# Corner sums of two samples in one GpSimd operation, and fewer comparisons on ScalarE, in the deformable stage of a metaformer kernel

## Chip, cores and metric

The kernel runs on one core of one Trainium2 chip. The metric is the device time of one execution in microseconds; the median of several runs is given. The engines are TensorE (PE in the profile; PEld is its weight load), VectorE (DVE), ScalarE (ACT), GpSimd (POOL) and SyncE (SP), each with its own queue of instructions; they wait for each other by semaphores.

## Reference

The model has four blocks, each a convolutional mixer and a feed-forward part, on x of shape (8, 64, 16, 16). The change lies in the mixer of the second block, a deformable convolution:

```
y = _layernorm(x)
h = conv3x3(y, w1) + b1;  offset = conv3x3(h, w2) + b2        # 4 groups x 9 taps x (dy, dx)
py = dy + ky + row;  px = dx + kx + column                    # sampling points
val = gather(y0, x0) * (wy0 * wx0) + gather(y0, x0 + 1) * (wy0 * wx1) \
    + gather(y0 + 1, x0) * (wy1 * wx0) + gather(y0 + 1, x0 + 1) * (wy1 * wx1)
x = x + relu(einsum('ogck,bgckhw->bohw', wr, val))
```

There are 4 groups x 9 taps = 36 sampling points ("samples") for each of the 8 x 256 = 2048 pixels, and each sample takes 16 channels at its 4 corners. Everything before and after this stage is the same in both kernels.

## The kernel before, in words

The 2048 pixels are 16 tiles of 128 (TILES = 16). A gather is made by TensorE as a matrix product with a one-hot matrix: for each sample, the index of its upper left corner (0 to 255, of an image's 256 pixels) is broadcast to all 128 partitions as a row of 2048 numbers (BC, four buffers, copied by SyncE from DRAM, L890), and compared with the partition's number. One comparison makes the one-hot for pixels 0 to 127 (the lower, qh = 0), another for pixels 128 to 255 (the upper, qh = 1); OH has three buffers (NOH = 3) of both.

- VectorE, `compare(s)` (L1095 to L1101), makes the lower comparison of each sample, and both where s % 3 is 0. One comparison is one tensor_scalar (is_equal) of 128 x 2048 fp16.
- ScalarE makes the upper comparison where s % 3 is 1 or 2, in two activations: DIST = |BC - q| (L1037) and OH = relu(1 - DIST) (L1040). `scalars(s)` is the number of samples up to s that ScalarE makes, and the value of the semaphore scalar_oh for which TensorE, SyncE and ScalarE wait.
- TensorE, `gather(s)` (L945 to L959), multiplies: 64 matmuls for a sample into two PSUM banks (4 and 5, or 6 and 7, by s % 2). It waits for the one-hots and for weigh(s - 2), which frees the banks.
- VectorE, `weigh(s)` (L1103 to L1112), multiplies the gathered values by the corner weights, two tensor_tensor of 128 x 512 from PSUM, into U, a pair of buffers (the tensors SQ and SD) by s % 2. It waits for gather(s) and, for the buffer, for GpSimd's sum of sample s - 2.
- GpSimd adds the four corners in two steps for each sample: V (V1, L903), 512 elements in each partition, then VAL (L906), 256 elements.
- After each eight samples TensorE transposes VAL in `contract` (L975), ScalarE evacuates it to VTA in `evac` (L1029), and TensorE multiplies it by the weights wd in `project` (L984). contract(n) stands after gather(11), (19), (27), (35), with contract(4) at the end; evac(n) stands on ScalarE after sample 13, 21, 29, and at the end.

Each engine's order is written out by hand. VectorE's is: compare(0), compare(1), the corner weights, then for s = 0 to 35: compare(s + 1) (not for s = 0), weigh(s). TensorE's is: gather(s), with contract and project where named. ScalarE can run ahead of the gathers by the three buffers of OH (its second activation waits for gather(s - 3)); SyncE refills BC(s) once both comparisons of sample s - 4 are made.

Of the kernel before, what the change touches and what calls it, by code (L numbers as in the profile page):

```python
# [11 lines left out]
ALU = mybir.AluOpType  # L12
ACT = mybir.ActivationFunctionType
F32 = mybir.dt.float32
# [5 lines left out]
P = 128  # L20
# [3 lines left out]
COLS = NB * PIX  # L24
HC = COLS // 2
TILES = B * PIX // P
# [7 lines left out]
SAMPLES = 36  # L34
CG = 16
# [37 lines left out]
def build(nc, x_dram, packs, idx_dram, out_dram):  # L73
    with ExitStack() as ctx:
        def sb(name, shape, dt=F32, where=None):
            return (where or ctx).enter_context(nc.sbuf_tensor(name, shape, dt))
# [3 lines left out]

        X = sb("X", [P, COLS])
        Y = sb("Y", [P, COLS])
        SQ = sb("SQ", [P, COLS])
        SD = sb("SD", [P, COLS])

        wconst = sb("wconst", [P, WIDTH[0]])
        wbuf = [sb(f"wbuf{i}", [P, max(w for n, w in enumerate(WIDTH) if n and n % 2 == i)]) for i in range(2)]
# [3 lines left out]
        def bank(n, cols=512):  # L91
            return PS[:, n * 512:n * 512 + cols]

        def wt(name, a=0, n=None, p0=0, p1=P):
            s, at, cols = AT[name]
            n = cols - a if n is None else n
            return wsb[s][p0:p1, at + a:at + a + n]
# [26 lines left out]
        def after_pool(eng, ins):  # L124

            steps["pool"] += 1
            ins.then_inc(pool_step, 1)
            eng.wait_ge(pool_step, steps["pool"])
# [13 lines left out]
        def ln_pe(pe, n):  # L142
            for h in range(2):
                pe.matmul(bank(h), wt("center"), X[:, h * HC:(h + 1) * HC], start=True, stop=True).then_inc(ln_centered, 1)  # L144
            for h in range(2):
                pe.wait_ge(ln_squared, 2 * n + h + 1)
                for q in range(4):
                    mm = pe.matmul(bank(2 + h, P)[32 * q:32 * q + 32, :], wt("mean32"), SQ[:, h * HC + q * P:h * HC + (q + 1) * P],
                                   start=True, stop=True, tile_position=(0, 32 * q))
                mm.then_inc(ln_var, 1)  # L150
            for h in range(2):
                pe.wait_ge(ln_rstd, 2 * n + h + 1)
                for q in range(4):
                    mm = pe.matmul(bank(2 + h)[:, q * P:(q + 1) * P], wt("spread", q * P, P), SD[:, h * P:(h + 1) * P],  # L154
                                   start=True, stop=True)
                mm.then_inc(ln_spread, 1)

        def ln_act(act, n, eps):
            if n == 0:
                warm(act, ACT.Sqrt)  # L160
            for h in range(2):
                act.wait_ge(ln_centered, 2 * n + h + 1)
                act.activation(SQ[:, h * HC:(h + 1) * HC], bank(h), ACT.Square).then_inc(ln_squared, 1)  # L163
            for h in range(2):
                act.wait_ge(ln_var, 2 * n + h + 1)
                act.activation(SD[:, h * P:(h + 1) * P], bank(2 + h, P), ACT.Sqrt, bias=wt(eps)).then_inc(ln_sd, 1)

        def ln_dve(dve, n, out_of):
# [6 lines left out]
            for h in range(2):  # L175
                c = slice(h * P, (h + 1) * P)
                dve.wait_ge(ln_sd, 2 * n + h + 1)
                dve.reciprocal(SD[:, c], SD[:, c]).then_inc(ln_rstd, 1)  # L178
            for h in range(2):
# [8 lines left out]
        def images(a):  # L188
            return a.rearrange("p (b r w) -> p b r w", b=2, r=H)
# [18 lines left out]
        with ExitStack() as sctx, nc.Block() as block:  # L208
# [60 lines left out]
            @block.sync  # L269
            def _(sp):  # L270
                xv = x_dram.rearrange("(g b) c p -> g c b p", g=2)
                for g in range(2):
                    sp.dma_start(X[C * g:C * g + C, :].rearrange("c (b p) -> c b p", b=NB), xv[g]).then_inc(x_in, 16)
                for n in range(3):
                    load_weights(sp, n)
# [557 lines left out]
        with ExitStack() as sctx, nc.Block() as block:  # L833
# [23 lines left out]

            def scalars(s):

                return s - s // 3  # L860
            BC = sb("BC", [P, NBC, TILES * P], FP16, sctx)
            OH = sb("OH", [P, NOH, 2, TILES * P], FP16, sctx)
            DIST = sb("DIST", [P, TILES * P], FP16, sctx)
            scalar_oh = sem("s3_scalar_oh")

            U = [a[:, :].rearrange("p (t k c) -> p t k c", t=TILES, k=4) for a in (SQ, SD)]
            V1 = sb("V1", [P, TILES, 2, CG], F32, sctx)
            VAL = sb("VAL", [P, 2, TILES, 8, CG], F32, sctx)
            (y_pad, c1_ps, h_in, tents_ready, c2_ps, gx_ps, gx_hi, gx_done, idx_ready, frac_ready, idxt_ps, idxt_in, idx_out,
             oh_ready, ga_ps, u_ready, val_ready, vt_ps, vt_in, dc_ps, xs_ready) = (  # L870
# [24 lines left out]
            @block.gpsimd  # L895
            def _(pool):
                pool.memset(YP[:, :, :], 0.0).then_inc(y_pad, 1)
                for k in range(3):
                    pool.memset(HS3[k][:, :, :], 0.0).then_inc(y_pad, 1)
                for s in range(SAMPLES):  # L900

                    pool.wait_ge(u_ready, s + 1)
                    after_pool(pool, pool.tensor_tensor(V1[:, :, :, :], U[s % 2][:, :, 0:2, :], U[s % 2][:, :, 2:4, :], ALU.add))  # L903
                    if s >= 16 and s % 8 == 0:
                        pool.wait_ge(vt_ps, 4 * (s // 8 - 1))
                    pool.tensor_tensor(VAL[:, (s // 8) % 2, :, s % 8, :], V1[:, :, 0, :], V1[:, :, 1, :], ALU.add).then_inc(val_ready, 1)  # L906
                    pool.wait_ge(val_ready, s + 1)

            @block.tensor
            def _(pe):  # L910
# [88 lines left out]
            @block.scalar  # L999
            def _(act):  # L1000
                ln_act(act, 2, "epsc")
                act.wait_ge(w_in[3], 16)
                act.wait_ge(y_pad, 4)
                for h in range(2):
                    act.wait_ge(c1_ps, h + 1)
                    for k in range(3):

                        a, b = max(0, 1 - k), min(W, W + 1 - k)
                        act.activation(pair(HS3[k], h, 2, 0)[:, :, :, a:b], images(bank(4 + h))[:, :, :, a + k - 1:b + k - 1],
                                       ACT.Identity, bias=wt("c1b")).then_inc(h_in, 1)  # L1010
                for n in range(2 * NB):
                    bl, qh = n // 2, n % 2
                    act.wait_ge(gx_ps, n + 1)
                    act.activation(GX[:, 0, qh, bl, :, :], bank(n % 4).rearrange("p (k c) -> p k c", k=4), ACT.Copy,
                                   scale=GSCALE).then_inc(gx_hi, 1)
                for g in range(NB):
                    act.wait_ge(idxt_ps, g + 1)
                    act.activation(IDXT[:, g * HC:(g + 1) * HC], bank(g).bitcast(FP16)[0:SAMPLES, 0:HC], ACT.Copy).then_inc(idxt_in, 1)

                act.wait_ge(frac_ready, 1)  # L1020
                for u, at in ((U0, 0.0), (U1, -1.0)):
                    after_act(act, act.activation(u[:, :, :], PY[:, :, :], ACT.Abs, bias=at if at == 0.0 else wt("minus1")))
                    act.activation(u[:, :, :], u[:, :, :], ACT.Relu, bias=1.0, scale=-1.0).then_inc(tents_ready, 1)

                def evac(ch):
                    rows = P if ch < 4 else 64
                    for q in range(4):
                        act.wait_ge(vt_ps, 4 * ch + q + 1)
                        act.activation(VTA[0:rows, ch % 4, q * 512:(q + 1) * 512], bank(q % 2)[0:rows, :], ACT.Copy).then_inc(vt_in, 1)  # L1029
                for s in range(SAMPLES):  # L1030

                    if s % 3:
                        act.wait_ge(bc_in[s % NBC], 16 * (s // NBC + 1))
                        if scalars(s - 1):

                            act.wait_ge(scalar_oh, scalars(s - 1))
                        after_act(act, act.activation(DIST[:, :], BC[:, s % NBC, :], ACT.Abs, bias=wt("negq1")))  # L1037
                        if s >= NOH:
                            act.wait_ge(ga_ps, s - NOH + 1)
                        act.activation(OH[:, s % NOH, 1, :], DIST[:, :], ACT.Relu, bias=1.0, scale=-1.0).then_inc(scalar_oh, 1)  # L1040
                    if s >= 13 and s % 8 == 5:
                        evac(s // 8 - 1)
                evac(3)
                evac(4)

                warm(act, ACT.Sqrt)

            @block.vector
            def _(dve):
# [7 lines left out]
                for n in range(2 * NB):  # L1057
                    bl, qh = n // 2, n % 2
# [10 lines left out]
                for g in range(NB):  # L1069
                    t = slice(4 * g, 4 * g + 4)  # L1070
# [24 lines left out]
                def compare(s):  # L1095
                    dve.wait_ge(bc_in[s % NBC], 16 * (s // NBC + 1))
                    if s >= NOH:
                        dve.wait_ge(ga_ps, s - NOH + 1)
                    for qh in range(1 if s % 3 else 2):
                        ins = dve.tensor_scalar(OH[:, s % NOH, qh, :], BC[:, s % NBC, :], wt("qidx", qh, 1), None, ALU.is_equal)  # L1100
                    ins.then_inc(oh_ready, 1)  # L1101

                def weigh(s):  # L1103
                    dve.wait_ge(ga_ps, s + 1)
                    if s >= 2:
                        dve.wait_ge(val_ready, s - 1)
                    for half in range(2):
                        o = U[s % 2][:, 8 * half:8 * half + 8, :, :].rearrange("p t k c -> p (t k) c")
                        src = bank(4 + 2 * (s % 2) + half).rearrange("p (k c) -> p k c", c=CG)
                        w = WC[:, s, 8 * half:8 * half + 8, :].rearrange("p t (k o) -> p (t k) o", o=1).broadcast_to([P, 32, CG])  # L1110
                        ins = dve.tensor_tensor(o, src, w, ALU.mult)  # L1111
                    ins.then_inc(u_ready, 1)  # L1112
# [8 lines left out]
                for bp in range(2):  # L1121
                    c = slice(bp * HC, (bp + 1) * HC)
# [900 lines left out]
```

## Time and profile before

| | us |
|---|---|
| median of 3 runs | 659.53 |
| lowest, highest | 659.16, 660.15 |
| the profiled execution | 663.59 |
| its span in the profile | 661.8 |

Times in the rows are microseconds from the start of the span unless marked ns. A timeline row gives start, duration, engine, line, operation, written tile <- read tiles, shapes, how many instructions were merged into the row (x2), and in brackets the idle time of the engine before it with what ended it. The page's second section shows the same as slices; the profiled execution is 4.1 us longer than the median of the plain runs, and the stage in question is about 122 us of it.

### The profile page before, as it was taken

What the parts mean: (1) busy time and instruction counts of PE and PEld (TensorE: products, weight loads), DVE (VectorE), ACT (ScalarE), POOL (GpSimd) and SP (SyncE); (2) the same over time, 40 slices, a digit from 0 to 9 for tenths busy, and PEclk for the clock granted to TensorE, in tenths of its full rate; (3) what the DMA queues carried; (4) which work ended last, traced back from release to release, by engine and by line L of the source; (5) the groups of instructions that cost most, each with busy time, mean ns of one, the idle gap of its engine ahead of it and who ended that gap; (6) DMA issues with size and microseconds to landing.
All of it is one profiled execution on the core that took longest, in us unless ns stands there. A gap on an engine that the chain in (4) does not pass through costs nothing. (4 is left out here: it accounts for less than half of the span.)

```text
span 661.8 us, 11669 instructions
## 1 busy us (share of the span) xinstructions
PE 555.0 (84%) x4942; PEld 297.8 (45%) x4942; DVE 352.8 (53%) x579; ACT 288.3 (44%) x395; POOL 148.6 (22%) x148
## 2 busy tenths in 40 slices
PE   3999999977899998487887867767997888799994
PEld 1544367844322467477777733233333334322221
DVE  2439902045455334787875837565235696632434
ACT  2633122223653231899998746443662011233221
POOL 9800000002000200298886920006003002000000
PEclk9999999999899999789997997796899999799998
DMA  7000000002000000655553100100002000000000
GB/s 270 2 2 2 1 0 1 0 1 93 1 0 1 29 0 10 221 195 171 195 183 130 66 16 1 45 8 30 0 0 104 0 0 1 0 1 1 0 17 16
DMA packets 7844, 30.09 MB, mean 45 GB/s; under 512 B 864, under 2 KB 2032, under 8 KB 7408
## 3 DMA queue, kind: packets, MB, share of 16 engines
q1 hardware_dynamic: 7792, 29.34, 12.7%
q8 instruction: 39, 0.64, 0.4%
q14 instruction: 13, 0.11, 0.0%
HBM read 28.67 MB, written 0.67 MB: 44 GB/s over the span
## 5 line engine op out<-in xcount | busy, mean ns | idle before, releaser
L958 PE MATMUL PS<-GX,OH 128*128 128x64 f16 x2304 | 76.0, 197 | 24.0 <-DVE OH L1100 16.1
L958 PEld LDWEIGHTS PS<-GX,OH 128*128 128x128 f16 x2304 | 73.9, 101 | 28.3 <-DVE OH L1100 19.5
L1037 ACT ACTIVATE DIST<-BC,wbuf 128x2048 f16<-128x2048 f16 x24 | 48.0, 2001 | 5.1 <-DMA BC<-idx_dram 3.3
L1821 DVE TENSOR_SCALAR HID<-PS,wbuf 128x512 f32<-128x512 f32 x32 | 23.8, 750 | 48.5 <-PE PS L1720 48.5
L1040 ACT ACTIVATE OH<-DIST 128x2048 f16<-128x2048 f16 x24 | 45.9, 1911 | 1.7 <-PE PS L958 1.0
L1100 DVE TENSOR_SCALAR OH<-BC,wbuf 128x2048 f16<-128x2048 f16 x48 | 42.6, 911 | 5.5 <-DMA BC<-idx_dram 5.5
L903 POOL TENSOR_TENSOR V<-SQ 128x512 f32<-128x512 f32 x18 | 27.5, 1527 | 67.9 <-DVE SQ L1111 66.8
L399 PE MATMUL PS<-T,DG 128*32 128x512 f32 x384 | 41.6, 593 | 0.7 <-DVE T L604 0.7
L144 PE MATMUL PS<-X,wconst 128*128 128x512 f32 x32 | 20.9, 786 | 22.6 <-DMA wconst<-pack_dram 8.9
L610 DVE SCALAR_TENSOR_TENSOR D<-QKVP,wbuf,D 128x1024 f32<-128x1024 f32 x27 | 34.5, 1285 | 8.9 <-ACT D L524 8.1
L163 ACT ACTIVATE SQ<-PS 128x512 f32<-128x512 f32 x16 | 9.6, 597 | 66.5 <-PE PS L144 66.5
L906 POOL TENSOR_TENSOR VAL<-V 128x256 f32<-128x256 f32 x36 | 37.0, 1027 | 2.8
L1760 ACT ACTIVATE HID<-PS,wbuf 128x512 f32<-128x512 f32 x32 | 21.9, 684 | 34.9 <-PE PS L1720 34.2
L1731 PE MATMUL PS<-HID,wbuf 128*64 128x512 f32 x128 | 36.1, 617 | 1.0 <-DVE HID L1821 1.0
L1716 PE MATMUL PS<-Y,wbuf 64*128 64x512 f32 x128 | 36.0, 639 | 0.7 <-ACT OMASK L1754 0.7
L1111 DVE TENSOR_TENSOR SQ<-PS,WC 128x512 f32<-128x512 f32 x36 | 23.1, 684 | 18.3 <-PE PS L958 16.2
L826 DVE TENSOR_TENSOR HS<-PS,HID 128x512 f32<-128x512 f32 x32 | 20.5, 686 | 20.0 <-PE PS L711 20.0
L690 POOL MEMSET CWT<- 128x2048 f32 x1 | 1.8, 1806 | 123.1 <-POOLq L208 123.1
L903 POOL TENSOR_TENSOR V<-SD 128x512 f32<-128x512 f32 x18 | 26.4, 1467 | 3.5 <-DVE SD L1111 2.3
L778 ACT ACTIVATE HID<-PS,wbuf 128x512 f32<-128x512 f32 x32 | 20.1, 682 | 14.0 <-PE PS L703 13.9
L399 PEld LDWEIGHTS PS<-T,DG 128*32 128x32 f32 x384 | 13.5, 110 | 27.8 <-issue 27.8
L388 PE MATMUL PS<-wbuf,D 128*128 128x256 f32 x96 | 25.7, 411 | 0.0
(304 smaller groups left out, 997.5 us busy)
## 6 DMA issues: line engine op xcount, KB each, us to landing
BC<-idx_dram SPq DMA_DIRECT2D x36, 512.0 KB, 4.0
wbuf<-pack_dram SPq DMA_DIRECT2D x1, 2468.0 KB, 11.8
wbuf<-pack_dram SPq DMA_DIRECT2D x1, 1656.0 KB, 7.2
wbuf<-pack_dram SPq DMA_DIRECT2D x1, 1494.5 KB, 6.1
wbuf<-pack_dram SPq DMA_DIRECT2D x1, 820.0 KB, 13.3
wbuf<-pack_dram SPq DMA_DIRECT2D x1, 732.0 KB, 3.9
wbuf<-pack_dram SPq DMA_DIRECT2D x1, 602.5 KB, 3.8
wconst<-pack_dram SPq DMA_DIRECT2D x1, 567.5 KB, 6.6
```

Source lines behind the costliest of these rows:

```text
L388: pe.matmul(half, src, w, start=(j == 0), stop=False)
L399: mm = pe.matmul(bank(DBANK[j] + n)[32 * q:32 * q + 32, :], DG[:, (2 * j + hf) * NBLK + i, :], src, start=(i == blocks[0]), stop=(i == blo ...
L610: ins = dve.scalar_tensor_tensor(out=d, in0=window(QKVP[j], dy, dx), scalar=wt("dw5", j * 25 + 5 * dy + dx, 1), in1=d, op0=ALU.mult, op1=A ...
L903: after_pool(pool, pool.tensor_tensor(V1[:, :, :, :], U[s % 2][:, :, 0:2, :], U[s % 2][:, :, 2:4, :], ALU.add))
L906: pool.tensor_tensor(VAL[:, (s // 8) % 2, :, s % 8, :], V1[:, :, 0, :], V1[:, :, 1, :], ALU.add).then_inc(val_ready, 1)
L958: mm = pe.matmul(o, OH[:, s % NOH, qh, t * P:(t + 1) * P], src, start=(qh == 0 and part == 0), stop=(qh == 1 and part == 1))
L1037: after_act(act, act.activation(DIST[:, :], BC[:, s % NBC, :], ACT.Abs, bias=wt("negq1")))
L1040: act.activation(OH[:, s % NOH, 1, :], DIST[:, :], ACT.Relu, bias=1.0, scale=-1.0).then_inc(scalar_oh, 1)
L1100: ins = dve.tensor_scalar(OH[:, s % NOH, qh, :], BC[:, s % NBC, :], wt("qidx", qh, 1), None, ALU.is_equal)
L1716: pe.matmul(bank(2 + (n + bh) % 4), wt("w1_3", e * FH3 + m * P, P, r, r + C), Y[r:r + C, bp * HC:(bp + 1) * HC], start=True, stop=False, t ...
L1731: pe.matmul(bank(bp)[C * bh:C * bh + C, :], wt("w2_3", (2 * e + m) * C, C), HID[:, (n + i) % 4, :], start=(e == 0 and m == 0), stop=False) ...
L1821: dve.tensor_scalar(HID[:, n % 4, :], bank(2 + n % 4), wt("b1_3", 2 * e + m, 1), 0.0, ALU.add, ALU.max).then_inc(hid_in_v, 1)
```

## The change

GpSimd's sums are made for two samples in one operation: `BATCHES` is (0, 2), (2, 2), ..., (32, 2), (34, 1), (35, 1). V of a batch of two has 1024 elements in each partition and VAL 512. For this U has two buffers of two samples each (SQ and SD, now one tensor SQSD, and a new tensor U_1) and V1 is twice as large. GpSimd waits for weigh of the later sample of its batch; weigh(s) waits for the batch before the last to be summed. The division of the upper comparisons goes from s % 3 to s % 5: VectorE makes both comparisons where s % 5 is 0 or 3 (15 samples instead of 12), ScalarE the upper one of the other 21 (instead of 24).

```diff
-        SQ = sb("SQ", [P, COLS])
-        SD = sb("SD", [P, COLS])
+        SQSD = sb("SQSD", [P, 2 * COLS])
+        SQ, SD = SQSD[:, 0:COLS], SQSD[:, COLS:2 * COLS]
...
-                return s - s // 3
+                return sum(1 for i in range(s + 1) if i % 5 not in (0, 3))
...
-            U = [a[:, :].rearrange("p (t k c) -> p t k c", t=TILES, k=4) for a in (SQ, SD)]
-            V1 = sb("V1", [P, TILES, 2, CG], F32, sctx)
+            U = [SQSD[:, :].rearrange("p (s t k c) -> p s t k c", s=2, t=TILES, k=4), sb("U_1", [P, 2, TILES, 4, CG], F32, sctx)]
+            V1 = sb("V1", [P, 2, TILES, 2, CG], F32, sctx)
+            BATCHES = [(s, 2) for s in range(0, SAMPLES - 2, 2)] + [(SAMPLES - 2, 1), (SAMPLES - 1, 1)]
...
-                for s in range(SAMPLES):
-
-                    pool.wait_ge(u_ready, s + 1)
-                    after_pool(pool, pool.tensor_tensor(V1[:, :, :, :], U[s % 2][:, :, 0:2, :], U[s % 2][:, :, 2:4, :], ALU.add))
+                for s, n in BATCHES:
+                    u = U[s // 2 % 2][:, s % 2:s % 2 + n].rearrange("p s t k c -> p (s t) k c")
+                    v = V1[:, 0:n].rearrange("p s t k c -> p (s t) k c")
+
+                    pool.wait_ge(u_ready, s + n)
+                    after_pool(pool, pool.tensor_tensor(v, u[:, :, 0:2, :], u[:, :, 2:4, :], ALU.add))
                     if s >= 16 and s % 8 == 0:
                         pool.wait_ge(vt_ps, 4 * (s // 8 - 1))
-                    pool.tensor_tensor(VAL[:, (s // 8) % 2, :, s % 8, :], V1[:, :, 0, :], V1[:, :, 1, :], ALU.add).then_inc(val_ready, 1)
-                    pool.wait_ge(val_ready, s + 1)
+                    v = V1[:, 0:n].rearrange("p s t k c -> p t s k c")
+                    pool.tensor_tensor(VAL[:, (s // 8) % 2, :, s % 8:s % 8 + n, :], v[:, :, :, 0, :], v[:, :, :, 1, :],
+                                       ALU.add).then_inc(val_ready, n)
+                    pool.wait_ge(val_ready, s + n)
...
-                    if s % 3:
+                    if s % 5 not in (0, 3):
...
-                    for qh in range(1 if s % 3 else 2):
+                    for qh in range(2 if s % 5 in (0, 3) else 1):
...
-                    if s >= 2:
-                        dve.wait_ge(val_ready, s - 1)
+                    if s >= 4:
+                        dve.wait_ge(val_ready, s // 2 * 2 - 2)
                     for half in range(2):
-                        o = U[s % 2][:, 8 * half:8 * half + 8, :, :].rearrange("p t k c -> p (t k) c")
+                        o = U[s // 2 % 2][:, s % 2, 8 * half:8 * half + 8, :, :].rearrange("p t k c -> p (t k) c")
```

## Rows read from the trace of the kernel before

**Rows 1.** The page: its span and the engines' busy times.
```profile
span 661.8 us, 11669 instructions
PE 555.0 (84%) x4942; PEld 297.8 (45%) x4942; DVE 352.8 (53%) x579; ACT 288.3 (44%) x395; POOL 148.6 (22%) x148
```
**Rows 2.** Slices of the stage: engines' busy us (instructions), then granted clock, DMA.
```profile
core 0: us, PE busy (x) PEld busy (x) DVE busy (x) ACT busy (x) POOL busy (x), PEclk, DMA share, GB/s
270.00:300.00 30.00, 23.52 (x671) 22.94 (x672) 26.82 (x37) 28.68 (x15) 21.50 (x17) 0.88 0.59 205
300.00:330.00 30.00, 23.58 (x649) 21.18 (x644) 23.90 (x35) 28.74 (x20) 26.16 (x21) 1.00 0.50 178
330.00:360.00 30.00, 23.27 (x580) 21.06 (x581) 20.77 (x29) 28.10 (x20) 24.09 (x20) 0.93 0.50 179
```
**Rows 3.** Groups by line, 269 to 392 us: busy, mean ns, idle before.
```profile
L958 PE MATMUL PS<-GX,OH 128*128 128x64 f16 x2304 | 76.0, 197 | 24.0 <-DVE OH L1100 16.1 <-ACT OH L1040 5.9 <-issue 2.0
...
L906 POOL TENSOR_TENSOR VAL<-V 128x256 f32<-128x256 f32 x36 | 37.0, 1027 | 2.8
```
**Rows 4.** ScalarE's timeline: first pairs, third evacuation, its waits, last activation.
```profile
270.44 2.00 ACT L1037 ACTIVATE DIST<-BC,wbuf 128x2048 f16<-128x2048 f16 x1 [2.04 <-DMA BC<-idx_dram]
...
274.48 2.00 ACT L1037 ACTIVATE DIST<-BC,wbuf 128x2048 f16<-128x2048 f16 x1
...
355.67 1.06 ACT L1029 ACTIVATE VTA<-PS 128x512 f32<-128x512 f32 x2
...
361.79 1.91 ACT L1040 ACTIVATE OH<-DIST 128x2048 f16<-128x2048 f16 x1 [0.99 <-PE PS L958]
...
369.01 2.00 ACT L1037 ACTIVATE DIST<-BC,wbuf 128x2048 f16<-128x2048 f16 x1 [1.27 <-DMA BC<-idx_dram]
...
375.08 1.91 ACT L1040 ACTIVATE OH<-DIST 128x2048 f16<-128x2048 f16 x1
```
**Rows 5.** VectorE's timeline, from windows of different width (x1 first, x2 both).
```profile
289.71 1.29 DVE L1111 TENSOR_TENSOR SD<-PS,WC 128x512 f32<-128x512 f32 x2 [0.60 <-PE PS L958]
...
295.28 0.74 DVE L1100 TENSOR_SCALAR OH<-BC,wbuf 128x2048 f16<-128x2048 f16 x1
...
295.28 1.89 DVE L1100 TENSOR_SCALAR OH<-BC,wbuf 128x2048 f16<-128x2048 f16 x2
...
317.79 1.29 DVE L1111 TENSOR_TENSOR SD<-PS,WC 128x512 f32<-128x512 f32 x2 [0.69 <-POOL VAL L906]
...
338.94 1.17 DVE L1100 TENSOR_SCALAR OH<-BC,wbuf 128x2048 f16<-128x2048 f16 x1
...
338.94 2.86 DVE L1100 TENSOR_SCALAR OH<-BC,wbuf 128x2048 f16<-128x2048 f16 x2
...
379.92 1.29 DVE L1111 TENSOR_TENSOR SD<-PS,WC 128x512 f32<-128x512 f32 x2 [0.87 <-POOL VAL L906]
```
**Rows 6.** GpSimd's timeline: additions beside comparisons, and the last ones, alone.
```profile
295.37 1.26 POOL L906 TENSOR_TENSOR VAL<-V 128x256 f32<-128x256 f32 x1
...
317.77 1.27 POOL L903 TENSOR_TENSOR V<-SQ 128x512 f32<-128x512 f32 x1
...
338.83 0.73 POOL L906 TENSOR_TENSOR VAL<-V 128x256 f32<-128x256 f32 x1
339.64 1.61 POOL L903 TENSOR_TENSOR V<-SQ 128x512 f32<-128x512 f32 x1
...
382.06 1.25 POOL L903 TENSOR_TENSOR V<-SD 128x512 f32<-128x512 f32 x1
383.39 0.73 POOL L906 TENSOR_TENSOR VAL<-V 128x256 f32<-128x256 f32 x1
```
**Rows 7.** TensorE's timeline: a gather at each clock, and an idle time.
```profile
270.64 3.40 PE L958 MATMUL PS<-GX,OH 128*128 128x64 f16 x64 [7.80 <-DVE OH L1100]
...
302.75 2.03 PE L958 MATMUL PS<-GX,OH 128*128 128x64 f16 x64 [1.61 <-ACT OH L1040]
...
356.31 1.97 PE L975 MATMUL PS<-wconst,VAL 128*128 128x128 f32 x8 [2.72 <-ACT VTA L1029]
```
**Rows 8.** Groups of GpSimd over the whole span: its longest addition.
```profile
L320 POOL TENSOR_TENSOR D<-wbuf,BK 96x768 f32<-96x768 f32 x1 | 1.5, 1539 | 0.1
```
**Rows 9.** The page's DMA issues: KB each, us to landing.
```profile
BC<-idx_dram SPq DMA_DIRECT2D x36, 512.0 KB, 4.0
```

## The prediction, made before the changed kernel was timed

> **What bounds the kernel now.** Everything that is changed lies in one stage, the deformable convolution, from about 269 to 391 us of a span of 661.8 us [rows 1]; so the first look is at the busy time of each engine in slices of that stage. ScalarE is busy 28.7 of 30 us there, GpSimd 26.2, TensorE 23.6, VectorE 23.9 [rows 2]. The second look is ScalarE's own timeline: from 270.44 it starts a comparison (a DIST and an OH activation) every 4.04 us, 24 of them, broken by three evacuations of VTA, to 377.0 (375.08 + 1.91) [rows 4]. 24 x 4.04 = 97.0 us; the evacuations take 2.3, 2.6 and 3.1; it waits 0.99 and 1.27 us; together 105 to 106.5 us. It is full, and sets the pace of the stage: 106.5 / 36 = 2.96 us for each sample. Lines say the same from the other side: the matmuls of the gather are only 76.0 us busy and wait 24.0 us for one-hots [rows 3].
>
> The third look is at what lies right behind ScalarE. GpSimd makes a sample's sums in 1.25 us (V) and 0.73 us (VAL) where it is alone, yet the mean VAL is 1027 ns [rows 3, 6]. The timelines of VectorE and GpSimd side by side show why. A comparison of VectorE (L1100) takes 0.74 us at 295.28; a second follows at once and the pair takes 1.89, not 1.41 us [rows 5]. The VAL of GpSimd issued at 295.37 took 1.26 us, to 296.63 [rows 6], and VectorE's second comparison could only finish 0.54 us later, at 297.17. At 338.94 both kinds of wait are seen: the first comparison takes 1.17 us since VAL is under way until 339.56; then V, issued at 339.64, holds to 341.25, and the second comparison ends at 341.80, 0.55 us later [rows 5, 6]. The reading: a comparison of VectorE and an addition of GpSimd exclude each other for their whole length, and GpSimd, if it stands waiting when the first of two comparisons ends, goes ahead of the second. There are 12 double comparisons; sample 0's, before GpSimd starts, takes 1.41 us, and each of the other 11 takes 1.88 us or more, with GpSimd's addition between the two. The weighing (L1111, from PSUM) isn't touched: 1.29 us for its two instructions at 317.79, beside a V of 1.27. The Trainium skill, "SBUF — State Buffer", section "Who interferes with whom", states this as a rule: the first of the two to issue holds the shared pair for its whole instruction. The rows agree, and what it does to the change is the forecast below.
>
> **The change part by part.**
> ScalarE: samples with s % 5 in 1, 2, 4 instead of s % 3 in 1, 2, that is 21 pairs instead of 24: 3 x 4.04 = 12.1 us less on the engine that sets the pace [rows 4].
> VectorE: three comparisons more, 51 instead of 48: 3 x 0.67 (0.74 less the overlap of neighbours) = 2.0 us, before waits.
> GpSimd: 17 batches of two samples and two of one. An addition costs 0.73 us for 256 and 1.25 for 512 elements: 0.2 fixed and 2.05 to 2.1 ns for each element [rows 6]. So V of 1024 is 2.35 us and VAL of 512 is 1.27: 3.6 for two samples instead of 3.96, and two gaps of 0.08 fewer, 17 x 0.5 = 9 us less. The trace has no addition of 1024; the nearest, 768 elements, took 1539 ns [rows 8], which gives at least 2.05 us; from above, no fixed part saved, 2.5 us. I take 2.35, which the two sizes of this very line give. Without its start of some 0.15, V keeps VectorE's comparison out for 2.2 us instead of 1.1, and VAL for 1.15 instead of 0.57. The Trainium skill, "GPSIMD Engine Reference", section "3.1 Elementwise", has 4497 ns for 2048 elements, an estimate of 2.25 us for 1024; the sum would be some 1 us lower by it.
> The waits: weighing s now needs the batch before the last (two buffers of two samples), always done in time by the schedule below, which removes the 0.69 us waits on VAL [rows 5]. The copy BC(s) for s % 5 = 1 starts after ScalarE's sample s - 4, now one pair (4.04 us) ahead instead of two, against 4.0 us to land [rows 9]: 0 to 0.5 us each on ScalarE, hidden while ScalarE isn't the last.
>
> **The schedule.** VectorE's order is compare(s + 1), then weigh(s). I laid the samples with the durations above (weigh 1.20, gather 1.95 at the full clock [rows 7], pair 4.04), following each wait. Sample 3 shows the pattern: weigh(1) ends and releases the batch (0,1) while the first comparison of sample 3 runs; V of 2.2 us takes its turn behind it, and only then comes the second: a double comparison takes 3.44 us instead of 1.8. gather(3), its weighing and all behind it are late by 1.6 us. So it is for each odd double sample (3, 5, 13, 15, ...). For an even one (8, 10, 18, ...) V is mostly in flight when the first comparison comes (0.7 to 1.0 us), and VAL goes between the two (1.15): 3.0 to 3.2 us. Both kinds in the times of the schedule, samples 7 to 10: weigh(7) 297.7 to 298.9; comparison 9 at 298.9, so V(6,7), released at 299.0, holds 299.6 to 301.8; gather(8) ends 299.8, weigh(8) to 301.0; the first comparison of 10 waits from 301.0 to 301.8 and ends 302.4; VAL(6,7) holds to 303.5; the second ends 304.1; gather(10) 304.1 to 306.1, when weigh(9) (304.0), comparison 11 (305.2) and V(8,9) behind it (305.9 to 308.2) have already begun, into which comparison 12 runs at 307.3.
> Ten samples on VectorE: weighing 12.0; six single comparisons, four of 0.67, one of 0.77 and one of 1.3, together 4.75; two odd doubles 6.9; two even 6.2; waits for a gather's end 1.1: 31.0 us. ScalarE would need 6 x 4.04 + 1.25 x 2.3 = 27.1 for the same ten, GpSimd 18 + its waits for 14 comparisons of 0.56, or 26.7. So VectorE's chain of weighing, blocked comparison and gather becomes the bound.
> Before, weigh(5) began at 289.71, weigh(15) at 317.79 and weigh(35) at 379.92 [rows 5]: 90.2 us for thirty, 30.1 for ten. Now: weigh(5) at 291.3, thirty samples at 31.0 = 93.1, weigh(35) at 384.4, 4.5 us later. GpSimd then ends 3.5 us behind it (the last two batches are single), before 4.2 (383.39 + 0.73 - 379.92) [rows 6]. The end of the stage moves by 4.5 - 0.7 = 3.8 us. What follows (contract(4), the projection) is the same.
> The clock: the schedule is at the full clock. Before, the granted clock of slices was 0.88 and 0.93 [rows 2]; a gather takes 3.40 us at the half clock, 2.03 at the full one [rows 7], and the clock fell after TensorE idled for 2.72 us. ScalarE's two waits and its long third evacuation, 3.1 us, are what that cost. Now TensorE idles for 2.4 to 2.9 us at about every fifth sample, so I expect such falls at least as often; half the gathers lie on the chain: 2 us, between 0 and 6.
> Sum: 3.8 + 2.0 = 5.8 us. The profiled execution took 663.59 (span 661.8), the runs' median is 659.53; the difference goes onto the median: 665.3 us.
>
> **The rivals.**
> A, the change pays as the busy times suggest. Place: the comparison next to V. If VectorE's second comparison isn't kept waiting by the longer addition, VectorE's ten samples fall from 31.0 by two times 2.1 and two times some 1 to below 25, and ScalarE's 27.1 decides: it ends at 270.44 + 84.8 + 8 = 363.2 to 364.5, the tail adds 9.8 (gather(33) ends with the last pair, weigh(33) 1.2, a batch 3.8 and 0.5 of waiting, two single batches of 2.16), so 374 against 384.1: 9.6 us faster, 649.9. It decides once the waits of ten samples (8.3 us) fall by 3.9, that is V's hold from 2.2 to about 1.4 us. For it: ScalarE is the full engine now. Against it: every double comparison of the trace. 12%.
> B, it comes out even: V nearer to 2.05 (2 us less), fewer falls of the clock (2 us less), and some even doubles meeting no V (1.65 instead of 3.1 us, as one did in my schedule). 657.5 to 660.8, 14%.
> C, TensorE's idle times let its clock fall in nearly every period: each fall puts 1.4 us on a gather [rows 7], four to seven of these on the chain instead of the 1.4 that I count: 669 to 673. 12%.
> The forecast itself, 662 to 668.5: 62%.
> That the change doesn't do what it says is no case here: its operands are plain.
>
> **How the numbers follow.** The likeliest case gives 665.3. Leaving out A and the upper end of C leaves 657.5 to 670. A measurement of this kernel can tell about 0.2% (1.3 us) from no change. Faster by more: A and a quarter of B, 0.16; within: 0.10; slower: the rest, 0.74.
>
> **What would show it.** In the trace after: V at 2.35 us alone and about 2.8 behind a comparison; the second comparison of samples 3, 5, 13, 15 at 2.85 us; ScalarE with waits on gathers instead of being full; "DVE OH" as the releaser of the gathers with more than 16 us; GpSimd no busier than 85 us; its last VAL near 388 to 390. Wrong if those comparisons take 0.75 to 1.3 us, or if ScalarE is full again and ends near 364.

## The result

| | ratio to the kernel before | 95% interval | median us, runs |
|---|---|---|---|
| changed kernel | 1.0146 | 1.0100 to 1.0192 | 671.93, 4 (before: 659.84) |
| once more, other comparison | 1.0147 | 1.0119 to 1.0176 | 671.6, 6 (before: 661.21) |

The change makes the kernel slower by 1.5%. On the 659.53 us from which the prediction started, 1.0146 is 669.2 us: within its range (657.5 to 670), 0.8 us below the upper end; the median of the four plain runs itself, 671.93, lies above it. The profiled execution took 670.25 us, span 668.5, against 663.59 and 661.8 before. One of the six executions of the second row was in a slower state (677.83 us, granted clock 0.940), and its ratio leaves it out.

The times of the four plain runs of the changed kernel go with the clock that TensorE was granted, as a mean over the run: 668.31 and 670.25 us at 0.949 and 0.947, 673.61 and 674.67 us at 0.939 and 0.937.

The page of the changed kernel: engines' busy time.

```profile
PE 556.3 (83%) x4942; PEld 298.2 (45%) x4942; DVE 373.1 (56%) x582; ACT 276.6 (41%) x389; POOL 133.7 (20%) x114
```

The repetition was made because the first interval is wide:

> The changed kernel itself, beside the others of this call on the same chip. Its first interval reached from 1.01 to 1.019 times the kernel before; by the others so far (V in two 1.0025, batches alone 1.0091) I expect 1.013 to 1.017.

In the busy times above ScalarE has 11.7 us less and GpSimd 14.9 us less to do than in [rows 1], as intended; VectorE has 20.3 us more. (A comparison or an addition that is kept out counts as busy while it waits.) The slices of the stage (columns as in [rows 2]) and the groups of lines between 266 and 400 us show which instruction has it:

```profile
270.00:300.00 30.00, 21.14 (x597) 20.48 (x595) 28.74 (x33) 25.53 (x14) 13.79 (x7) 0.90 0.53 175
300.00:330.00 30.00, 23.26 (x580) 21.16 (x576) 24.59 (x30) 22.77 (x15) 19.40 (x10) 0.89 0.48 162
330.00:360.00 30.00, 24.71 (x650) 21.56 (x647) 28.07 (x35) 23.60 (x16) 19.10 (x10) 0.94 0.47 160
```

```profile
L963 PE MATMUL PS<-GX,OH 128*128 128x64 f16 x2304 | 79.4, 200 | 33.9 <-DVE OH L1105 30.1 <-ACT OH L1045 2.6 <-issue 1.1
L1105 DVE TENSOR_SCALAR OH<-BC,wbuf 128x2048 f16<-128x2048 f16 x51 | 63.4, 1268 | 5.2 <-DMA BC<-idx_dram 5.1
L1042 ACT ACTIVATE DIST<-BC,wbuf 128x2048 f16<-128x2048 f16 x21 | 42.0, 2001 | 12.9 <-DMA BC<-idx_dram 11.9
```

The 51 comparisons of VectorE take 63.4 us, 1268 ns each, where before 48 took 42.6 us, 911 ns each (neighbours overlap a little, so the busy time is less than the sum); the gathers wait 30.1 us for them, in [rows 3] 16.1. ScalarE is no longer full: 22.8 to 25.5 us of 30 instead of 28.7.

The place itself, in the timelines of VectorE and GpSimd: a double comparison (both halves of a sample, on VectorE) behind the weighing of an odd sample (at 318 us), one behind the weighing of an even sample (at 301 us), and GpSimd's additions beside them.

```profile
300.74 2.98 DVE L1105 TENSOR_SCALAR OH<-BC,wbuf 128x2048 f16<-128x2048 f16 x2
...
317.74 0.74 DVE L1105 TENSOR_SCALAR OH<-BC,wbuf 128x2048 f16<-128x2048 f16 x1
...
317.74 3.49 DVE L1105 TENSOR_SCALAR OH<-BC,wbuf 128x2048 f16<-128x2048 f16 x2
```

```profile
292.78 2.40 POOL L906 TENSOR_TENSOR V<-SQSD 128x1024 f32<-128x1024 f32 x1 [2.76 <-DVE SQSD L1116]
...
301.63 1.54 POOL L910 TENSOR_TENSOR VAL<-V 128x512 f32<-128x512 f32 x1
...
317.97 2.70 POOL L906 TENSOR_TENSOR V<-SQSD 128x1024 f32<-128x1024 f32 x1 [2.42 <-DVE SQSD L1116]
```

The first comparison at 317.74 takes 0.74 us. V, issued at 317.97, ends at 320.67, and the second comparison ends at 321.23, 0.56 us after it. At 300.74 V is under way until 301.50, and VAL (301.63 to 303.17) goes between the two comparisons: 2.98 us. All eight doubles behind an odd weighing take 3.47 to 3.52 us, where [rows 5] show 1.89.

The chain that the page reports lies in the last stage, as before, and says nothing of this one.

### The profile page after: what moved, and what is told of

It reads as the page before. It is cut to its first block and busy times, and to the rows that moved or that the text cites. A ratio compares the mean times of both kernels' runs of the same rounds, so it can differ in the third digit from the quotient of the medians.

```text
span 668.5 us, 11621 instructions
## 1 busy us (share of the span) xinstructions
PE 556.3 (83%) x4942; PEld 298.2 (45%) x4942; DVE 373.1 (56%) x582; ACT 276.6 (41%) x389; POOL 133.7 (20%) x114
## 5 line engine op out<-in xcount | busy, mean ns | idle before, releaser
L963 PE MATMUL PS<-GX,OH 128*128 128x64 f16 x2304 | 79.4, 200 | 33.9 <-DVE OH L1105 30.1
L963 PEld LDWEIGHTS PS<-GX,OH 128*128 128x128 f16 x2304 | 76.7, 103 | 38.8 <-DVE OH L1105 34.4
L1105 DVE TENSOR_SCALAR OH<-BC,wbuf 128x2048 f16<-128x2048 f16 x51 | 63.4, 1268 | 5.2 <-DMA BC<-idx_dram 5.1
L1042 ACT ACTIVATE DIST<-BC,wbuf 128x2048 f16<-128x2048 f16 x21 | 42.0, 2001 | 12.9 <-DMA BC<-idx_dram 11.9
L1045 ACT ACTIVATE OH<-DIST 128x2048 f16<-128x2048 f16 x21 | 40.1, 1910 | 4.3 <-PE PS L963 3.7
L906 POOL TENSOR_TENSOR V<-SQSD 128x1024 f32<-128x1024 f32 x9 | 24.2, 2691 | 76.4 <-DVE SQSD L1116 76.4
L163 ACT ACTIVATE SQSD<-PS 128x512 f32<-128x512 f32 x16 | 9.6, 597 | 66.2 <-PE PS L144 66.2
L906 POOL TENSOR_TENSOR V<-U 128x1024 f32<-128x1024 f32 (+1 forms) x10 | 24.4, 2444 | 19.3 <-DVE U L1116 19.3
L910 POOL TENSOR_TENSOR VAL<-V 128x512 f32<-128x512 f32 (+1 forms) x19 | 27.3, 1437 | 2.6
L1116 DVE TENSOR_TENSOR U<-PS,WC 128x512 f32<-128x512 f32 x36 | 23.1, 681 | 7.9 <-PE PS L963 7.9
```

Of the source, the lines that this page charges most:

```text
L906: after_pool(pool, pool.tensor_tensor(v, u[:, :, 0:2, :], u[:, :, 2:4, :], ALU.add))
L910: pool.tensor_tensor(VAL[:, (s // 8) % 2, :, s % 8:s % 8 + n, :], v[:, :, :, 0, :], v[:, :, :, 1, :], ALU.add).then_inc(val_ready, n)
L963: mm = pe.matmul(o, OH[:, s % NOH, qh, t * P:(t + 1) * P], src, start=(qh == 0 and part == 0), stop=(qh == 1 and part == 1))
```

## The experiments

Each was timed in five rounds beside the kernel before, in three comparisons. "Stage" is the time from the first weighing to the second update of X in one profiled execution: 114.5 us before (275.86 to 390.37), 123.9 in the changed kernel (275.06 to 398.99). These 9.4 us agree with the ratio (9.6 us); the spans of the two profiled executions differ by only 6.7 us, since 2.7 us come out of stretches ahead of and behind the stage, in which nothing was changed. Differences in microseconds are taken from the ratios, on 659.53 us.

**The batches alone.** The old division (12 samples with both comparisons on VectorE), sums of two samples.

```diff
-                    if s % 5 not in (0, 3):
+                    if s % 3:
```

> The changed kernel with the old division of the upper comparisons (12 samples with both on VectorE, 24 on ScalarE); only GpSimd's batches of two stay. Theory (the longer hold of V keeps the second comparison of a double out): doubles are 11 behind GpSimd's start instead of 14, each still 2.4 to 3.5 us, so about 3 x 2 = 6 us less than the changed kernel, 662 to 666, still slower than before; doubles behind weigh of an odd sample still take 3.5 us. Rival (the three more comparisons on VectorE do the harm): at or under the time of before, 659 or less, since GpSimd has less to do.

Measured: 1.0091 (1.0068 to 1.0113), 6.0 us slower than before. A comparison of VectorE takes 1174 ns:

```profile
L1105 DVE TENSOR_SCALAR OH<-BC,wbuf 128x2048 f16<-128x2048 f16 x48 | 55.3, 1174 | 5.4 <-DMA BC<-idx_dram 5.4
```

So the larger part of the loss, 6.0 of 9.7 us, comes with the batches alone and not with VectorE's three more comparisons; 665.5 us is within the expectation. Six of its twelve doubles take 3.48 to 3.51 us, as the eight behind an odd weighing do in the changed kernel. The remaining 3.7 us come with the three more doubles; the expectation had put some 6 us on them.

**The division alone.** The kernel before with s % 5 in its three places, sums of one sample.

> The kernel before with only the division s % 5 (15 doubles on VectorE, 21 samples on ScalarE); GpSimd sums each sample by itself. Theory: doubles stay at 1.9 us, GpSimd's additions and all comparisons together take 36 x 2.16 + 51 x 0.56 = 106 us, against 105 before, so nothing is gained from the 12 us taken off ScalarE and little is lost: 658 to 663. Rival (the division does the harm): 665 or more. Second rival (ScalarE alone was the bound): 650 to 654.

Measured: 0.9952 (0.9928 to 0.9976), and in the repetition:

> The kernel before with the division s % 5 alone, once more, since its gain (0.9952, 0.9928 to 0.9976) is small. Expected 0.993 to 0.998.

0.9948 (0.9926 to 0.9970): faster than both kernels, by 3.3 us. A comparison takes 915 ns, as before, though three more are made, the stage 110.2 us:

```profile
L1100 DVE TENSOR_SCALAR OH<-BC,wbuf 128x2048 f16<-128x2048 f16 x51 | 45.4, 915 | 5.6 <-DMA BC<-idx_dram 5.6
```

The rival that the division does harm has fallen. I had expected 658 to 663 us and no gain, since GpSimd's additions and all comparisons together come to 106 us; 0.9952 is 656.4 us, so that was a miss. A part of ScalarE's 12.1 us is gained, 3.3 of them.

The traces show where. VectorE's weighings waited 16.8 us for gathers before and 7.5 in the division alone; against these 9.3 us stand 1.2 us more of waits for VAL and 2.8 us more of comparisons. That leaves 5.3 us, and from the first to the last weighing it is 98.7 us instead of 104.1. The longest single wait before, 6.65 us, was behind the third evacuation of VTA, for which TensorE waited 2.72 us [rows 7]; in the division alone TensorE waited 1.28 us for it, and the same weighing 1.69 us:

```profile
361.73 1.29 DVE L1111 TENSOR_TENSOR SQ<-PS,WC 128x512 f32<-128x512 f32 x2 [6.65 <-PE PS L958]
```

About 1 us of this is lost again behind the last weighing, 11.6 us to the end of the stage instead of 10.5.

The half of the change that takes load off the full engine pays by itself; the batches cost 6.0 us by themselves and 13 on top of the division.

**V of a batch in two additions.** Same wait for two samples, same VAL of 512; only the one addition of 1024 is now two of 512.

```diff
-                    after_pool(pool, pool.tensor_tensor(v, u[:, :, 0:2, :], u[:, :, 2:4, :], ALU.add))
+                    for i in range(n):
+                        w = slice(TILES * i, TILES * i + TILES)
+                        ins = pool.tensor_tensor(v[:, w], u[:, w, 0:2, :], u[:, w, 2:4, :], ALU.add)
+                    after_pool(pool, ins)
```

> The changed kernel with V of a batch made by two additions of 512 elements instead of one of 1024, under the same wait; VAL stays one of 512. Theory (the length of one hold is what counts): the second comparison of a double behind an odd weighing takes 1.7 us instead of 2.8, 8 times, so 8 to 10 us less than the changed kernel: 659 to 663. Rival (the late release, waiting for two samples, does the harm): no better than the changed kernel, 669 or more, since GpSimd's work grows by 17 x 0.2 us.

Measured: 1.0025 (1.0005 to 1.0045), 8 us less than the changed kernel, with one more addition in each batch for GpSimd. The eight doubles behind an odd weighing take 2.40 to 2.43 us instead of 3.47 to 3.52, here that of sample 15 (V is two additions merged into one row):

```profile
313.13 2.41 DVE L1108 TENSOR_SCALAR OH<-BC,wbuf 128x2048 f16<-128x2048 f16 x2
313.36 3.32 POOL L908 TENSOR_TENSOR V<-SQSD 128x512 f32<-128x512 f32 x2 [0.57 <-DVE SQSD L1119]
```

The second comparison gets its turn after the first of the two additions (1.1 us) and not after both. So the length of one addition accounts for 8 of the 13 us that the batches cost on top of the division. The rival, that the late release of a batch does the whole harm, has fallen; 5 us against the division alone (1.0025 and 0.995) are left, and this run doesn't say what they are due to.

**TensorE's idle times filled.** The changed kernel with 40 small matmuls ahead of the gathers of eleven double samples (not 0, 3, 20 and 28), into a PSUM bank that is free then; they are in no result.

```diff
+                    if s >= 5 and s % 5 in (0, 3) and s % 8 != 4:
+                        if s >= 12:
+                            pe.wait_ge(vt_in, 4 * ((s - 12) // 8 + 1))
+                        for _ in range(FILL):
+                            pe.matmul(bank(0)[:, 0:64], IDH[:, :], GX[:, 0, 0, 0, :, 0:CG], start=True, stop=True)
                     pe.wait_ge(oh_ready, s + 1)
```

> The changed kernel with 40 more small matmuls (about 1.2 us) into an unused PSUM bank ahead of the gathers of double samples, where TensorE otherwise idles for 2 to 3 us; they are in no result. If the falls of TensorE's clock in these idle times cost some 4 us more than the full-clock schedule, as the trace after suggests, the granted clock of the stage is 1.0 nearly throughout and the time falls by 3 to 5 us, to 665 to 668. If the clock costs nothing on the chain, the time stays or rises by up to 1 us for each gather that the filling delays.

Measured: 1.0086 (1.0060 to 1.0112), 4.0 us less than the changed kernel. The granted clock (the third number from the end) is 1.00 from 300 us on:

```profile
300.00:330.00 30.00, 26.64 (x782) 24.42 (x779) 26.99 (x33) 24.30 (x17) 20.93 (x10) 1.00 0.51 173
330.00:360.00 30.00, 26.66 (x752) 24.09 (x750) 28.88 (x34) 24.84 (x16) 21.20 (x10) 1.00 0.50 177
```

VectorE's comparisons are unchanged here (63.2 us); from the first to the last weighing it is 109.4 us (276.43 to 385.79), in the changed kernel 114.2 (275.06 to 389.24). VectorE's weighings wait 7.6 us for gathers instead of 12.3: these 4.7 us are nearly the whole of the 4.8 by which the chain is shorter.

**V by sample, VAL by two.** V is released by each weighing, as before; only VAL is made for two samples.

```diff
+                        pool.wait_ge(u_ready, s + i + 1)
                         ins = pool.tensor_tensor(v[:, w], u[:, w, 0:2, :], u[:, w, 2:4, :], ALU.add)
```

> The changed kernel with V of each sample released by its own weighing (one addition of 512, as before), and VAL of two samples in one addition of 512. Theory (length of one hold, and its place behind a weighing): V of the earlier sample now falls beside other work, so a double behind an odd weighing meets one V of 512 (1.1 us) and an even one meets V or VAL; comparisons are busy some 50 us in all; 0.3 to 0.8% under V in two, so 0.995 to 1.001 times before. Rival (batching as such, four buffers and a late VAL, costs something besides the hold): 1.0025 or more, as with V in two.

Measured: 1.0017 (0.9992 to 1.0041), stage 114.4 us. The expectation was 0.995 to 1.001, so a miss at its edge: comparisons took 56.0 us, not 50, and an earlier V brought no gain over V in two that the intervals show. The same with the old division:

> The same with the old division (12 doubles on VectorE, 24 samples on ScalarE). Theory: ScalarE is full again, 24 x 4.04 us and the evacuations, so whatever GpSimd saves (some 4 us) can't be used: 0.998 to 1.004 times before, no better than the one with 21 samples on ScalarE. Rival (the division matters nothing, only GpSimd's total): equal to the one with 21, at 0.995 or less.

Measured: 1.0029 (1.0003 to 1.0054), within the expectation, but not told apart from the other, so the division's own effect is not seen here. Against the division alone (0.9952) they are 0.65% and 0.77% slower. What differs from it is the VAL of 512 elements, made after the second V, which keeps a comparison out for some 1.15 us instead of 0.57, and the four buffers; the buffers are cleared below.

**Weighing between the two comparisons.** A double sample's upper comparison comes after weigh(s), so that GpSimd's addition may run beside the weighing.

```diff
                     weigh(s)
+                    if 1 <= s < SAMPLES - 1 and (s + 1) % 5 in (0, 3):
+                        upper(s + 1)
```

> The changed kernel with the two comparisons of a double sample parted: lower, weigh(s), upper, so that GpSimd's long addition falls beside the weighing, which needs no shared port. Theory: for 14 doubles the wait of the upper comparison falls by up to 1.2 us each, but weigh(s) waits for its gather first, which takes back a part: mean of a comparison 1.0 us or less instead of 1.27, 4 to 8 us less than the changed kernel, 1.003 to 1.009 times before. Rival (the wait of VectorE isn't what sets the pace): no change against the changed kernel, or slower by the later one-hots.

Measured: 1.0301 (1.0257 to 1.0344), 10 us slower than the changed kernel. My theory's number was wrong (it said 1.003 to 1.009), and the last words of the rival right. Comparisons did fall, but only from 63.4 to 59.0 us (44.9 + 14.1, the upper halves of the doubles in a line of their own); six times the lower comparison of the next sample now stood behind the addition and took 2.83 to 2.87 us:

```profile
L1104 DVE TENSOR_SCALAR OH<-BC,wbuf 128x2048 f16<-128x2048 f16 x36 | 44.9, 1247 | 5.4 <-DMA BC<-idx_dram 5.4
...
L1121 DVE TENSOR_TENSOR SQSD<-PS,WC 128x512 f32<-128x512 f32 x36 | 23.1, 684 | 17.3 <-PE PS L963 17.2
...
L1121 DVE TENSOR_TENSOR U<-PS,WC 128x512 f32<-128x512 f32 x36 | 23.1, 684 | 9.3 <-PE PS L963 9.2
...
L1111 DVE TENSOR_SCALAR OH<-BC,wbuf 128x2048 f16<-128x2048 f16 x15 | 14.1, 939 | 0.0
```

But now gather(s + 1) waits for a comparison that waits for weigh(s) and so for gather(s): for these samples TensorE and VectorE work in turn instead of side by side. VectorE's weighings wait 26.4 us for gathers (17.2 into SQSD, 9.2 into U) instead of 12.3. That is 14.1 us more, against 4.4 less of comparisons; from the first to the last weighing it is 123.4 us instead of 114.2. How much of the 26.4 us is due to the clock, 0.77 from 270 to 300 us, was not separated.

**Four buffers without batches, and filling the faster kernel.** Two attempts to go beyond the division alone: weigh(s) waits for the sum of s - 4 (`BATCHES` of one sample each in the changed kernel); and 24 small matmuls ahead of the gathers of doubles.

> Sums of one sample in one operation, the division s % 5, but the changed kernel's four sample buffers in U, so that weigh(s) waits for the sum of s - 4 instead of s - 2. In the trace of the division alone VectorE waits 7.0 us for VAL. If these waits are on the chain: 3 to 7 us less than the division alone, 0.985 to 0.992 times before. If they only move the wait to the next comparison (GpSimd's additions and the comparisons exclude each other in any order): within 0.3% of the division alone.

> The division alone with 24 small matmuls more (0.7 us) into an unused PSUM bank ahead of the gathers of double samples; they are in no result. In the trace of the division alone TensorE idles 1.7 us there and the granted clock of three of four slices is 0.88 to 0.94. If these falls cost what they did in the changed kernel: the clock is 1.0 and the time 0.2 to 0.4% under the division alone. If not: no change.

Measured: 0.9931 (0.9905 to 0.9958) and 0.9941 (0.9918 to 0.9964), against 0.9948 for the division alone in the same comparison. Neither is told apart from it. With four buffers the waits for VAL are gone, but VectorE's 51 comparisons take 49.5 us instead of 45.4: most of the wait has only moved to the next comparison. With the filling the granted clock is 1.00 in three slices of four instead of one, and nothing that the intervals show is gained. Between the first and the last weighing the division alone had a single fall, at 325 us, behind an idle time of 1.84 us; with the filling this stretch takes 100.1 us instead of 98.7, with 46.9 us of comparisons instead of 45.4, and what follows up to the end of the stage 9.8 us instead of 11.6.

## Why the prediction was right, and where its size was off

**The bound and the mechanism: right.** The forecast was that the longer addition of GpSimd keeps the second of two comparisons out and makes VectorE's chain the bound in ScalarE's place. It named 3.44 us for a double behind an odd weighing, of which the trace has eight at 3.47 to 3.52, and 3.0 to 3.2 for the others, of which it has 2.98, 2.99, twice 3.33, 2.42 and 1.77. V of 1024 elements was put at 2.35 us from the two sizes of [rows 6]; where it was nearly alone it took 2.40. The batches alone lost 6.0 us; splitting the addition gave 8 of 13 us back. The hand-over, in the forecast a reading of 11 doubles, is thereby shown. The rule of the Trainium skill, "SBUF — State Buffer", section "Who interferes with whom", is that the first to issue holds the pair for its whole instruction; the V of 2.70 us at 317.97, which the second comparison waited out, agrees with it.

**The schedule: right within 1 us.** Laid at the full clock it had 108.5 us from the first to the last weighing (275.86 to 384.4). The kernel with the idle times filled, whose clock stays full from 300 us on, takes 109.4. Part of this agreement is luck: the six other doubles took 16.8 us together where the schedule would have 18.0 to 19.2, and the weighings waited 7.6 us for gathers where it has 1.1 for ten samples, some 4 in all.

**The clock: mis-sized, and this is nearly the whole miss.** I added 2.0 us, with bounds 0 and 6. From the first to the last weighing the changed kernel takes 114.2 us, 5.7 more than the schedule. TensorE's timeline has five falls there (281.69, 303.79, 321.28, 347.05 and 385.73), and an idle time without one (297.46):

```profile
281.69 5.45 PE L963 MATMUL PS<-GX,OH 128*128 128x64 f16 x128 [1.87 <-DVE OH L1105]
...
297.46 3.91 PE L963 MATMUL PS<-GX,OH 128*128 128x64 f16 x128 [2.41 <-DVE OH L1105]
303.79 5.35 PE L963 MATMUL PS<-GX,OH 128*128 128x64 f16 x128 [2.42 <-DVE OH L1105]
...
321.28 3.29 PE L963 MATMUL PS<-GX,OH 128*128 128x64 f16 x64 [2.92 <-DVE OH L1105]
...
347.05 2.87 PE L963 MATMUL PS<-GX,OH 128*128 128x64 f16 x64 [2.56 <-DVE OH L1105]
...
385.73 3.48 PE L963 MATMUL PS<-GX,OH 128*128 128x64 f16 x64 [2.90 <-DVE OH L1105]
```

At the full clock two gathers take 3.91 us and one 2.03 to 2.04, so four of the falls put 1.4, 1.3, 0.8 and 1.5 us on the gather of a double sample (the last four). VectorE's waits for these gathers grew by as much: the weighings at 307.31, 324.61, 349.96 and 389.24 waited 1.72, 1.53, 1.10 and 2.37 us, with the idle times filled 0.28, 0.28, 0.28 and 0.94. That is 4.9 us. Of the 1.5 us of the fall at 281.69 only 0.4 reached a weighing (that at 284.16 waited 0.67 us instead of 0.28). Together 5.3 to 5.4 us lie on the chain; the remaining 0.3 of the 5.7 is error of the schedule.

The step that was mis-sized is "half the gathers lie on the chain", which left 1.4 falls. Four of the falls came with the gather of a double, and there it was on the chain each time: once its comparisons and the weighing ahead are done, VectorE has one comparison left and then stands waiting for this gather. With 5.7 for 2.0 the sum is 3.8 + 5.7 = 9.5 us; 1.0146 is 9.6. Filling took back 4.0 of it, the fillers' own delays included. What came is thus the forecast's mechanism with the falls of rival C, whose 669 to 673 holds 669.2; the forecast's own 662 to 668.5 doesn't, though the intervals of the two ratios reach down to 666 and 667 us. The wide range held the number because it took in the lower end of C.

**Rival A fell**, by the batches: its condition, V's hold at 1.4 us or less, was met by no kernel with the addition of 1024. V in two additions has holds of 1.1 us and was still no faster than before (1.0025): its comparisons fell by 7.0 us in all, 2 for ten samples, where A needed 3.9. In part A was right about the division, which alone gives 3.3 us.

**The waits for copies.** For BC I had 0 to 0.5 us each, hidden. ScalarE waited 11.9 us, 10.0 without the wait ahead of its first pair, up to 2.5 at a time: SyncE refills a buffer after VectorE's comparison too, and that is late now. The forecast had named waits for gathers as the sign; those were 3.7 us. TensorE waited only 2.6 us for ScalarE's one-hots, so the copies were hidden nevertheless, but the size was wrong.

**What stays open.** Why VAL by two and V by sample loses 0.6% against the division alone was not separated further; the longer VAL between two comparisons is argued from its length. Nor does any run say what makes the clock fall behind one idle time and not behind another: 2.42 us had a fall and 2.41 had none, 1.87 had one, and in the kernel with the weighing in between 2.92 us (at 326.61) had none.

## What to carry to other kernels

Where two engines keep each other out, as GpSimd's additions and VectorE's comparisons do here, fusing small operations on one of them saves its own fixed cost (here 0.5 us for two samples) and doubles the time for which the other must stand still (1.1 to 2.2 us). Look at what is queued there right behind the release, and count the longer wait once for each such place. Try the parts of a change one by one: here one half gained 0.5% and the other turned the whole into a loss of 1.5%. And where a change lengthens TensorE's idle times ahead of work that the chain waits for, count a fall of the clock there at its full price, here 0.8 to 1.5 us each, and not at half; four of the five gathers behind 2.4 us or more had one.

## What the runs showed of the hardware

- With two VectorE comparisons back to back and a GpSimd addition waiting, GpSimd went between them each time: 3.47 to 3.52 us for eight doubles, whose comparisons alone take 1.41.
- A GpSimd addition of two fp32 inputs took 0.73 us for 256 elements in each partition, 1.27 for 512 and 2.40 for 1024 (the shortest of 17; a comparison ran beside its first 0.17 us): 0.2 us fixed and 2.1 to 2.2 ns for each element.
- TensorE's granted clock fell to half (a gather of 64 matmuls up to 3.48 us instead of 2.03) at four of the five gathers behind idle times of 2.41 to 2.92 us, and at one behind 1.87 us; with 40 small matmuls in eleven of the idle times (1.33 us each) it stayed full from 300 us to the end of the stage.
